# Grouped feed-forward: a copy-out ring of eight buffers, and scatters queued two blocks behind the gathers' turn

## The reference, cut to what matters

```python
scores = softmax(x @ gate_w.T)                    # 16 experts
topk_w, topk_idx = top_k(scores, 4); topk_w /= sum(topk_w)
y = sum over experts e of cw[:, e] * ((silu(x @ wg[e].T) * (x @ wu[e].T)) @ wd[e].T)   # 176 inner columns
return y + shared_mlp(x)                          # 352 inner columns
```

## Time and profile before

| | |
|---|---|
| median of three runs | 1484.31 us |
| the profiled execution, its own time | 1483.01 us |
| its span, first to last instruction | 1481.2 us |
| mean granted TensorE clock, share of full speed | 0.953 |
| PE busy | 1309.8 us (88%) |
| DVE busy | 1042.3 us (70%) |
| ACT busy | 852.7 us (58%) |
| POOL busy | 851.5 us (57%) |

### The profile page before, as it was taken

The page is one execution under the profiler, slowest core; times in us unless marked ns, Lnnn a source line. Parts: engine busy times, 40 slices in busy tenths (PEclk is TensorE's granted clock), DMA queues, the critical chain, the costliest instruction groups (busy, mean ns, idle before and its releaser), DMA issues.

```text
span 1481.2 us, 28548 instructions
## 1 busy us (share of the span) xinstructions
PE 1309.8 (88%) x8106; PEld 1098.7 (74%) x8106; DVE 1042.3 (70%) x2544; ACT 852.7 (58%) x2102; POOL 851.5 (57%) x752
## 2 busy tenths in 40 slices
PE   5999999999978986659999999899999998978893
PEld 3888888888877874547777777677777778877882
DVE  5676666646677546348888888788888887677545
ACT  1444444464436543248787878677878875436552
POOL 3555555530345772357787877677778650445772
PEclk9999999999979998869999999899999999979996
DMA  3000000002336335221222222122222202335334
GB/s 117 26 26 27 27 26 25 16 13 69 120 106 189 113 105 208 50 50 44 65 55 65 55 66 57 37 52 70 52 65 51 58 1 78 123 115 196 96 105 171
DMA packets 52271, 110.72 MB, mean 75 GB/s; under 512 B 11616, under 2 KB 21408, under 8 KB 51872
## 3 DMA queue, kind: packets, MB, share of 16 engines
q1 hardware_dynamic: 40992, 82.22, 19.3%
q0 software_dynamic: 9024, 24.65, 5.6%
q10 hardware_dynamic: 2112, 2.10, 0.4%
HBM read 64.11 MB, written 15.47 MB: 54 GB/s over the span
## 4 chain that ended last, share of the span: by engine, by line
PE 42%; issue 20%; POOL 17%; DVE 12%; DMA 4%; ACT 3%; POOLq 0%; SPq 0%; DVEq 0%; ACTq 0%
PE ps L1466 28%; PE ps L1621 7%; POOL pb_odd L1106 4%; POOL yt L1106 3%; PE ps L1831 2%; POOL z L1106 2%; POOL rb L1091 2%; DVE rb L548 2%; DVE x_res L859 2%; DMA raw_w<-in_wx 2%; POOL pb_low L1106 2%; POOL ra L1095 2%; PE ps L1691 1%; PE ps L1719 1%; PE ps L1553 1%
## 5 line engine op out<-in xcount | busy, mean ns | idle before, releaser
L918 DVE TENSOR_TENSOR pt_lo<-ps,pt_hi 128x512 fp32r<-128x512 f32 (+3 forms) x384 | 205.5, 548 | 53.3 <-ACT pt_hi L1385 47.7
L1466 PE MATMUL ps<-kh,qh 128*128 128x512 f32 (+3 forms) x768 | 204.4, 376 | 20.8 <-DMA qh<-qt_hi 9.0
L1385 ACT CAST pt_hi<-ps 128x512 fp32r<-128x512 f32 (+3 forms) x384 | 178.8, 481 | 59.8 <-PE ps L1831 51.7
L903 DVE TENSOR_REDUCE nmb<-ps 128x1 f32<-128x1024 f32 (+7 forms) x256 | 191.7, 749 | 28.3 <-PE ps L1466 27.2
L1466 PEld LDWEIGHTS ps<-kh,qh 128*128 128x128 f32 x768 | 132.2, 196 | 44.1 <-issue 12.9
L1466 PE MATMUL ps<-pt_hi,vst 128*128 128x512 f32 (+3 forms) x384 | 156.5, 408 | 1.8 <-DVE ra L883 1.8
L1045 POOL DMA_INDIRECT z<-zbuf,gidx x94 | 97.2, 1034 | 83.0 <-DVE sidx L763 30.3
L1466 PE MATMUL ps<-pt_lo,vst 128*128 128x512 f32 (+3 forms) x384 | 132.7, 349 | 0.0
L1183 ACT ACTIVATE pa<-sma,nmax 128x192 f32<-128x192 f32 x128 | 57.3, 449 | 129.4 <-DVE nmax L585 105.2
L1010 POOL TENSOR_TENSOR pa<-pa,rinv 128x384 f32<-128x384 f32 x64 | 53.0, 828 | 130.6 <-DVE rinv L593 130.6
L1054 POOL DMA_INDIRECT ybuf<-yb,sidx x94 | 95.1, 1012 | 40.8 <-issue 24.5
(11 more groups left out here) (225 smaller groups left out, 4162.6 us busy)
## 6 DMA issues: line engine op xcount, KB each, us to landing
raw_w<-in_wx SPq DMA_DIRECT2D x36, 608.0 KB
rb<-raw SPq DMA_DIRECT2D x192, 64.0 KB, 2.0
yg<-ybuf SPq DMA_DIRECT2D x8, 1024.0 KB, 8.0
qh<-qt_hi SPq DMA_DIRECT2D x64, 128.0 KB, 2.3
qh<-qt_lo SPq DMA_DIRECT2D x64, 128.0 KB, 2.4
wa<-in_wa SPq DMA_DIRECT2D x16, 384.0 KB, 3.0
wb<-in_wb SPq DMA_DIRECT2D x8, 384.0 KB, 3.4
wo_a<-in_wo_a SPq DMA_DIRECT2D x16, 128.0 KB, 2.0
```

The source lines that it names most:

```text
L903: v.tensor_reduce(nmb[:, par, i:i + 1], ps[:, b:b + 2, :].rearrange("p b k -> p (b k)")[:, 0:P * (t + 1)], AX.X, ALU.max, negate=True).the ...
L918: v.tensor_tensor(pt_lo[:, s % 3, at], ps[:, 4 + s % 2, at], pt_hi[:, s % 3, at].bitcast(F32), ALU.subtract).then_inc(sem("b_pt_lo"), 1)
L1385: s_.copy(pt_hi[:, s % 3, at], ps[:, 4 + s % 2, at]).then_inc(sem("b_pt_hi"), 1)
L1466: return t_.matmul(o, l, r, start=start, stop=stop)
```

## The change

The ring `yb` has eight slots in place of four, so `y_out(b)` waits for the scatter of block b - 8. POOL's scatter of a block stands two turns behind its loop in place of four: `gather(b+8)`, then `scatter(b-2)`, and two scatters are left after the loop. The ring's 2048 numbers take the place of the old ring, `btri` and `xg_hole`, so nothing else moves; `btri` becomes a view of the ring's last slot. The `rope` load is issued by SP behind the four `yg` loads and no longer waits for the last gate-and-up product. The four semaphores of the `yg` loads are gone (the loads count on four older ones), which makes room for four more `sca`.

```diff
-YB_RING = 4
+YB_RING = 8
+SCATTER_LAG = 2
...
-            btri = sb("btri", [P, NE, NE], c=own)
-            sb("xg_hole", [P, 3 * D], c=own)
...
+        btri = yb[:, YB_RING - 1, :].rearrange("p (e f) -> p e f", e=NE)
...
-                        sem(f"{s}_yl{n}"), 16)
+                        sem(f"{s}_{BACK[n]}"), 16)
...
-            sp.wait_ge(sem("f_gu"), NM)
-            sp.dma_start(rope[:, :, :], d["rope_b"]).then_inc(sem("b_consts"), 16)
             sp.wait_ge(sem("f_down"), NM)
             sp.dma_start(maskb[:, :], d["maskb"]).then_inc(sem("b_consts"), 16)
             gather_back("f")
+            sp.dma_start(rope[:, :, :], d["rope_b"]).then_inc(sem("b_consts"), 16)
...
-                                dve.wait_ge(sem(f"{s}_yl{t0 // 2}"), since(s, f"yl{t0 // 2}") + 16)
+                                dve.wait_ge(sem(f"{s}_{BACK[t0 // 2]}"), F_TOTAL[BACK[t0 // 2]] * (1 + (s == "g")))
...
                     if b + XG_RING < NB:
                         gather(b + XG_RING)
-                    if b >= 4:
-                        scatter(b - 4)
-                for b in range(NB - 4, NB):
+                    if b >= SCATTER_LAG:
+                        scatter(b - SCATTER_LAG)
+                for b in range(NB - SCATTER_LAG, NB):
                     scatter(b)
...
+BACK = ("raw0", "raw1", "consts", "kc")
```

More of the change, by code:

```diff
@@ L2013, in uses @@
     return len(range(u, NB, ring))
+BACK = ("raw0", "raw1", "consts", "kc")
 F_TOTAL = {"ln": 2 * NT, "var": 2, "rstd": 2, "z": NT, "zt": 4, "xt_hi": 4, "xt_lo": 4,
-           "consts": 32, "kc": 32, "wg_hi": 1, "wg_lo": 1, "logits": 2, "chosen": 2, "rank": 2, "hot": 2,
-           "idx": 4, "route": 34, "ex": 1, "raw0": 16 * N_W // 2, "raw1": 16 * N_W // 2,
+           "consts": 48, "kc": 48, "wg_hi": 1, "wg_lo": 1, "logits": 2, "chosen": 2, "rank": 2, "hot": 2,
+           "idx": 4, "route": 34, "ex": 1, "raw0": 16 * N_W // 2 + 16, "raw1": 16 * N_W // 2 + 16,
            "w_hi": N_W, "w_lo": 2 * POOL_LO, "w_lod": N_W - POOL_LO, "zs": 32, "gu": NM, "silu": NM, "h": NM, "ht": NM,
@@ L2022 @@
 F_TOTAL.update({f"sca{u}": 16 * uses(u, YB_RING) for u in range(YB_RING)})
-F_TOTAL.update({f"yl{n}": 16 for n in range(NT // 2)})
 def since(s, name):
```

## The result

The changed kernel takes 1479.22 us (median of 20 runs, 1476.37 to 1486.20); the kernel before 1486.08 us over 20 runs. The ratio is 0.9963, 95% interval 0.9951 to 0.9974: 5.5 us saved (3.9 to 7.3 by the interval), where the prediction said 8.9 us and a time of 1475 us. The two medians differ by 6.9 us. The profiled execution took 1481.19 us (span 1479.2 us, 2.0 us less than before), so the two traces differ by less than the medians; the experiments show why one pair of traces can't be subtracted whole.

What follows compares the result with a forecast made beforehand. It took POOL's gather-scatter pairs, through copy-outs waiting on the four-slot ring, to bound both feed-forwards. Gains of 4.4 us in f and 4.5 in g, other parts 0, summed to 8.9 us: 1475 us, range 1470 to 1481.5.

Steps and rivals of the forecast that it cites:

- the ring: Both feed-forwards: with eight slots all ring waits go; PE done with its blocks 4.65 us earlier in f, 4.28 in g.
- The forecast of 4.5 us: Second feed-forward g: POOL's run ends with the last scatter at 1453.7 against 1458.22, so g gains 4.5 us.
- POOL's pace of 2.57 us a pair: Gather and scatter in POOL, start to start: 2.57 us a pair against PE's 2.20 a block, so POOL ends both stages.
- rivals 2 and 4: POOL's pair dearer, 2.65 us: 1479.5, chance 0.14; POOL's queue bounds at worse price, 2.9 us: 1493, chance 0.05.
- rival 3: Only labelled waits go, g's 2.50 us being PE's: g gains 1.1 us, f 4.4; 1478.5, chance 0.12.
- The four added waits: SP before the yg loads: waits on events long past, cost 0, at most 0.1 us a stage.
- when `rope` is first needed: Second attention: load issued near 570, landing by 585, first use at 599.57 or 595; ten microseconds hide it, cost 0.
- Gathers, the cover of both sums: End of f: gather 46 goes 3.9 us later, lands in time by 2.0 us, at worst late by 0.2; g much the same.
- Rival 5: Nothing gained but a microsecond: late landings stall gathers instead of copy-outs; 1482, chance 0.09.
- f's 4.65 us lost to the ring: First feed-forward, blocks 29 to 43: 14 blocks took 35.49 us where 30.84 were due; f's forecast gain was 4.4.
- 1.3 us of earlier start for scatter 13: First feed-forward: behind copy-out 13, scatter 13 goes at 493.23 in the new order, at 494.50 in the old one.

Runs made afterwards that it cites:

- e1: Changed kernel with the ring of eight kept but the scatter four turns behind as before: f 69.18 us, g 69.11, ratio to the kernel before 0.9950.
- b1: The kernel before, run again unchanged with its own trace: f 72.54 us, g 72.95, ratio 1.0010.
- e4: The kernel before with only the rope load moved behind the yg loads: f 71.72 us, g 74.25, ratio 1.0008.
- e0: The changed kernel run again, nothing altered: f 71.11 us, g 68.56, ratio to the kernel before 0.9961.
- e9: The changed kernel run a third time, nothing altered: f 70.86 us, g 68.84, ratio to the kernel before 0.9958.
- e3: Changed kernel with the wvb and wb loads issued behind the last gather's landing, their splits behind the last block: f 68.72 us, g 68.84, ratio 0.9952.
- e5: Changed kernel with scatter four turns behind, and wvb and wb loads and splits moved behind the last gather and block: f 68.67 us, g 69.05, ratio 0.9936.
- e7: The same kernel as e5, run again: f 68.85 us, g 69.26, ratio to the kernel before 0.9931.
- e8: Changed kernel with scatter four turns behind, and the wvb and wb loads also issued in g at block 39: f 68.98 us, g 69.31, ratio 0.9937.
- e2: The kernel before, ring of four, with only the scatter queued two turns behind: f 77.57 us, g 72.19, ratio 1.0005.
- e6: Changed kernel with the wvb and wb loads also issued in g at block 39: f 70.70 us, g 73.26, ratio to the kernel before 0.9966.

## Why the prediction was wrong

*Right:* the ring was what held the copy-outs, in g too, where the label said PE: e1 removes it with nothing else, and g falls from 73.4 us (mean of before, b1, e4) to 69.0 (mean of the eight ring-of-eight traces whose gathers met no loads there), 4.4 us. The forecast of 4.5 us was for the last scatter, though, and by that the changed kernel gained 4.0: from copy-out 14 to scatter 46, 74.65 us (before, b1, e4) against 70.65 (after, e0, e9). POOL's pace of 2.57 us a pair held to the hundredth (gathers 45 and 46 above), which puts rivals 2 and 4 out; rival 3 is out by the gain in g. POOL ended g, as forecast; in f PE did. The four added waits left nothing: the first `yg` load is issued 2.56 us behind the start of the last scatter, for 2.55 before. No slowing of the first `yg` load by `rope` shows either: DVE waited 4.66 us for it, for 4.53 and 4.66 in the two traces of the kernel before. The gather count was right too: gather 46 was forecast 56.1 us behind copy-out 14 and went 56.7 us behind it.

*Wrong, but cheap: when `rope` is first needed.* It came 12.85 us after issue, at 584.98. The forecast 585 was met by luck, from an earlier issue (570 for 572.13) and a longer landing (15 us). And the ten microseconds of room to its use by DVE, now at 597.75 (it answers to the earlier trace rows), weren't the room that counts. POOL's program waits for `rope` and `maskb` before the first `rstd` of the second attention:

```python
            w_lo_b(0)
            pool.wait_ge(sem("b_consts"), 32)
            norm("b", 0)
```

The chain of waits after, and what `rstd` needs and when it ran, first before, then after:

```profile
572.13 12.85 DMA rope<-in_rope_b
```

```profile
585.02 0.17 DVE L477 TENSOR_SCALAR var<-mv 128x4 f32<-128x4 f32 x1
585.34 1.15 POOL L984 TENSOR_TENSOR rstd<-var,negh 128x4 f32<-128x4 f32 x1 [12.95 <-DVE var L477]
```

```profile
582.97 0.17 DVE L476 TENSOR_SCALAR var<-mv 128x4 f32<-128x4 f32 x1
585.05 1.36 POOL L983 TENSOR_TENSOR rstd<-var,negh 128x4 f32<-128x4 f32 x1 [14.84 <-DMA rope<-in_rope_b]
...
597.75 0.69 DVE L882 TENSOR_TENSOR ra<-ps,rope 128x512 f32<-128x512 f32 x1 [3.77 <-ACT raw L1346]
```

`rstd` started 1.9 us behind the end of `var`, where it took 0.15 us before. DVE had 3.2 us of other work in that time, so little of it is left further on: from the end of `var` to the second `rstd` it is 9.50 us before and 9.73 after, and 9.7 in every trace with `rope` behind the `yg` loads. The move cost 0.2 us, which the prediction put at nothing.

*Wrong:* the step "Gathers, the cover of both sums", in f. It took the landing from a stage in which gather and loads never met (3.4 us in the median, 5.6 at most), found 2.0 us of room, and called it in time. (The 5.6 us come from the stage's first part; the gathers issued behind block 13 landed in 3.9 us at most before, too.) It did not ask what else a stage that ends earlier would start earlier: SP's loads hang on block 39, not on the clock. They were 7.4 us behind the last gather before (554.55 against 547.18), and 1.6 us ahead of it after. The landing became 5.9 us and PE lost 70.8 - 68.9 = 1.9 us (mean of four traces with the change against mean of e1, e3, e5, e7, e8). Its price was wrong too, "each microsecond of lateness costs one": gather 46 landed when PE was about to turn it, and that step still took 0.85 us more than 2.20, 0.68 of it idle behind the turn. Rival 5, which had the stall move from the copy-outs to the gathers, came true for this part of f. In g nothing of it came.

*Mis-sized:* f's 4.65 us lost to the ring came from one trace. The mean of the three traces of that kind is 72.5, so with all of it removed the gain is 72.5 - 68.9 = 3.7 us, not 4.4. The waits are as irregular as the landings that cause them. Together: 72.5 - 70.8 = 1.7 us in f and 4.4 in g make 6.1 us to copy-out 46. POOL's late end of g takes some 0.5 of it and `rope` 0.2, which leaves 5.4, beside 5.5 measured; with an interval of 3.9 to 7.3 us that close a match is luck.

*A step that was needless in the change itself:* the text saw that scatter 13 starts the run in both orders and that the shorter lag only makes gathers later, and still took it as harmless. It counted 1.3 us of earlier start for scatter 13 and 0.6 came of it. e2 and e1 show the lag as cost without gain: the ring alone does as well to copy-out 46 of g, ends g 0.5 us sooner, and is 1.6 us better in f.

## What to carry to other kernels

When a stage gets faster, list every transfer that is issued on its progress, and lay the new times of all of them beside each other; a landing time measured while two transfers were apart says nothing of when they meet. A deeper ring takes irregular landings out of the path; queueing its writes a turn or two sooner brought nothing here, where the first of a back-to-back run waits for its own data anyway. When a load is moved, look in every engine's program for the wait on it: the first wait, and not the first use, says when it is needed. Measure a stage in three traces before putting its stalls into a sum.

## What the runs showed of the hardware

A POOL indirect DMA that waits for a copy-out starts late: copy-out 13 ended at 493.28 + 0.37 = 493.65, and its scatter started at 494.43, 0.78 us later, though POOL stood waiting. Each stage with two turns shows 0.78 or 0.79 us at this scatter. The prediction had 0.1 us, which it read from gather 25; but that gather waits for PE's turn of block 17, whatever the label says. By the sum it moved POOL's run later by 0.7 us and helped to make gather 46 meet the loads.

A turn that PE has to wait for costs more than the wait. Behind it PE sat idle once more before its next product, put down to issue: 0.52 us behind the turn of block 45 in the changed kernel's f, 0.53 and 0.52 in e6's g, 0.57 behind a turn in g before that had waited 1.28 us. The least behind a labelled wait of 0.4 us or more in any trace is 0.37 us (e2). Behind block 46's turn in the changed kernel's f it was 0.68, though no wait is labelled there. The cause isn't shown.

A stall of PE can be paid twice. In g of the kernel before, PE's row behind the weight split at block 12 and the stretch from there read (granted clock 0.50, third number from the end):

```profile
1377.02 0.95 PE L1466 MATMUL ps<-w_ex,gx_hi 128*128 x2 [2.71 <-DVE gx_lo L776]
```

```profile
1376.90:1382.00 5.10, 4.98 (x19) 4.92 (x20) 1.30 (x4) 1.44 (x4) 2.45 (x3) 0.50 0.26 80
```

That is the lower of TensorE's two levels, 1.2 GHz, behind a stall of 2.7 us in which PE did nothing. The stall itself is there in all 26 stages of the thirteen traces, 2.6 to 2.7 us long. Behind it the clock stood at 1.00 in seventeen, and copy-outs 12 to 14 took 7.0 to 7.3 us. It was 0.50 for 5 us in five (g of before, e0, e1 and e5, f of e4), which then took 9.7 to 9.8 us, and 0.66 in the mean of 5 us in four (f of e3, e7 and e8, g of e2), which took 8.5. The same kernel falls on either side (before against b1, the changed kernel against e0), so this is what one trace against another can show by chance at one place.
